# Four equal column strips in an elastic down-projection, and the expert attention's third and tail transposes moved ahead of V

## What is computed

```
m_small = sum(gumbel_weights[i] * _mlp_branch(ns2, w_fc1, b_fc1, w_fc2, b_fc2, C // ALPHA[i]) for i in range(3))
# _mlp_branch keeps the first C // ALPHA[i] = 192, 96, 64 channels at its input and at its output
h = jax.nn.gelu(xp * cmask @ w1 + b1, approximate=False)
return (h @ w2 + b2) * cmask
```

```
for e in range(wq.shape[0]):
    q = (x @ wq[e].T).reshape(b, s, nh, hd).transpose(0, 2, 1, 3)      # k, v alike
    scores = jnp.where(mask, jnp.einsum('bhqd,bhkd->bhqk', q, k) * scale, NEG)
    o = jnp.einsum('bhqk,bhkd->bhqd', jax.nn.softmax(scores, axis=-1), v)
    outs.append(o.transpose(0, 2, 1, 3).reshape(b, s, h) @ wo[e].T)
fused = jnp.concatenate(outs, axis=-1)
return jax.nn.silu(fused @ w_gate.T) * (fused @ w_up.T)
```

## Time and profile before

| | us |
|---|---|
| median of 3 runs | 1318.52 (1316.98 to 1318.92) |
| profiled execution | 1316.51 |
| its span (first to last instruction) | 1314.8 |
| mean granted TensorE clock | 0.922 of full |
| busy in the span: PE / PEld | 1190.5 (91%) / 939.6 (71%) |
| busy: ACT / DVE / POOL | 762.4 (58%) / 718.5 (55%) / 390.1 (30%) |

### The profile page before, as it was taken

One profiled execution on the slowest core, in us unless ns is written; L12 is line 12 of the kernel. 1 busy time (PEld: TensorE's weight loads), 2 busy tenths in 40 slices (PEclk: granted clock), 3 DMA queues, 4 the chain that ended last, 5 costly groups with the idle time before them and its releaser, 6 DMA issues. The chain is left out here.

```text
span 1314.8 us, 33568 instructions
## 1 busy us (share of the span) xinstructions
PE 1190.5 (91%) x13067; PEld 939.6 (71%) x13067; DVE 718.5 (55%) x2290; ACT 762.4 (58%) x3342; POOL 390.1 (30%) x529
## 2 busy tenths in 40 slices
PE   6789986999997699986899999999999999996898
PEld 5479954777774264324788898988889898883376
DVE  7345465666765113224667666666666666665200
ACT  1154534777773633313877777777777777873511
POOL 1100023433331433202443443444344344331000
PEclk8779976999997699966999999999999999996699
DMA  7000000000005300001000000000000000000000
GB/s 237 22 1 1 1 1 0 2 2 2 2 2 116 72 1 0 1 0 43 2 3 2 2 2 3 2 2 2 3 2 2 2 2 2 2 2 1 0 27 28
DMA packets 34732, 19.82 MB, mean 15 GB/s; under 512 B 24592, under 2 KB 32016, under 8 KB 34576
## 3 DMA queue, kind: packets, MB, share of 16 engines
q1 hardware_dynamic: 34432, 17.20, 4.9%
q10 hardware_dynamic: 144, 0.49, 0.1%
HBM read 15.12 MB, written 1.77 MB: 13 GB/s over the span
## 5 line engine op out<-in xcount | busy, mean ns | idle before, releaser
L1860 POOL TENSOR_TENSOR e_W<-e_W,e_RS 128x384 f32<-128x384 f32 x256 | 203.8, 827 | 348.7 <-DVE e_RS L1788 348.7
L1731 ACT ACTIVATE e_W<-banks,e_MX 128x128 f32<-128x128 f32 x768 | 268.9, 389 | 18.6 <-DVE e_MX L1776 18.5
L1731 ACT ACTIVATION_READ_ACCUMULATOR e_W<-banks,e_MX 128x1 f32 x768 | 175.9, 229 | 0.0
L1725 ACT COPY e_PT<-banks 128x512 f32<-128x512 f32 x128 | 69.0, 588 | 104.9 <-PE banks L1636 104.9
L1588 PE MATMUL banks<-XT,e_wqk 128*128 128x141 f32 x768 | 111.5, 296 | 11.8 <-DVE e_GU L1830 8.4
L1588 PEld LDWEIGHTS banks<-XT,e_wqk 128*128 128x128 f32 x768 | 97.8, 193 | 14.2 <-issue 11.6
L1636 PE MATMUL banks<-ident,e_W 128*128 128x128 f32 x768 | 105.5, 273 | 2.8 <-POOL e_W L1860 1.7
L1600 PE MATMUL banks<-e_wv,XT 128*128 128x192 f32 (+1 forms) x512 | 100.3, 339 | 0.1
L1636 PEld LDWEIGHTS banks<-ident,e_W 128*128 128x128 f32 x768 | 90.2, 141 | 6.3 <-POOL e_W L1860 2.0
L469 POOL TENSOR_TENSOR rstd<-veps,nhalf 128x6 f32<-128x6 f32 x15 | 20.6, 1372 | 242.6 <-DVE veps L435 242.6
L1117 POOL TENSOR_TENSOR f_W<-f_W,f_RS 128x423 f32<-128x423 f32 x64 | 56.3, 891 | 116.6 <-DVE f_RST L1101 108.7
(11 more groups left out here) (252 smaller groups left out, 2660.2 us busy)
## 6 DMA issues: line engine op xcount, KB each, us to landing
xp<-in_patches_dram SPq DMA_DIRECT2D x4, 768.0 KB, 8.6
H<-in_h_dram SPq DMA_DIRECT2D x1, 1728.0 KB, 10.8
out_dram<-H SPq DMA_DIRECT2D x6, 288.0 KB, 2.3
e_g<-in_e_gu_dram SPq DMA_DIRECT2D x1, 1536.0 KB, 8.1
e_o<-in_e_o_dram SPq DMA_DIRECT2D x4, 192.0 KB, 5.8
e_wqk<-in_e_qk_dram SPq DMA_DIRECT2D x8, 96.0 KB, 2.5
e_wqk<-in_e_qk_dram SPq DMA_DIRECT2D x24, 32.0 KB, 2.4
e_wv<-in_e_v_dram SPq DMA_DIRECT2D x4, 192.0 KB, 2.7
```

Of the source, the lines that this page charges most:

```text
L1725: nc.scalar.copy(PT[:, 4 * u:4 * u + 4, :], bank[4 + u][:, 0:4 * P]).then_inc(s_pa, 1)
L1731: ex = nc.scalar.activation(W[n % 2][:, t, :], bank[i][:, x * P:(x + 1) * P], ACT.Exp, bias=MX[:, t:t + 1], accum_out=SM[n % 2][:, t:t + 1])
L1860: nc.gpsimd.tensor_tensor(x, x, RS[n % 2][:, 3 * i:3 * i + 3].unsqueeze(2).broadcast_to([P, 3, P]), ALU.mult).then_inc(s_nm, 1)
```

## The change

Three edits. In `elastic_down` the 64-column matmul of variant 2 becomes two of 32 columns, in strips 0 and 1, with the same moving data; variants 1 and 0 stay in strips 2 and 3. In PE's list of the expert attention `project_v(n)` moves from behind `scores(n)` to behind `transpose_tail(n - 1)`. In DVE's list `evacuate_tail(n - 1)` moves up to behind `evacuate_weights(n - 1)`, and `evacuate_v(n)` moves down to behind the first reciprocals.

```diff
-                            for v, lo, n in ((2, 0, 64), (1, 64, 32), (0, 96, 32)):
-                                nc.tensor.matmul(t0[lo:lo + n, 0:GT_], m_w2[:, m, lo:lo + n], hid[g % 2][:, 3 * m + v, :],
+                            for v, lo in ((2, 0), (2, HP), (1, 2 * HP), (0, 3 * HP)):
+                                nc.tensor.matmul(t0[lo:lo + HP, 0:GT_], m_w2[:, m, lo:lo + HP], hid[g % 2][:, 3 * m + v, :],
                                                  start=(m == 0), stop=(m == HM - 1), tile_position=(0, lo),
                                                  skip_group_check=True)
...
                         if n < N:
                             scores(n)
-                            project_v(n)
                         if 1 <= n <= N:
                             pe.wait_ge(s_pa, 2 * n - 1)
                             pe.wait_ge(s_nm, 5 * n - 1)
...
                             transpose_tail(n - 1)
+                        if n < N:
+                            project_v(n)
                         if n >= 2:
                             out_project(n - 2)
...
                             maxima(n)
-                            evacuate_v(n)
                         if 1 <= n <= N:
                             evacuate_weights(n - 1)
+                            evacuate_tail(n - 1)
                         if n < N:
                             reciprocals(n, 0, 6, 2)
-                        if 1 <= n <= N:
-                            evacuate_tail(n - 1)
+                            evacuate_v(n)
```

## The result

The changed kernel takes 1284.18 us (median of 4 runs, 1278.96 to 1284.51) against 1318.35 us for the kernel before (4 runs, 1316.98 to 1318.92): a ratio of 0.9726, 95% interval 0.9702 to 0.9749, 2.7% faster. Forecast were 1289.6 us and a range of 1285 to 1298. The direction and both main mechanisms were right; the gain was larger, 34 us and not 29, and the time lies 0.8 us under the range. Of the 5.4 us, 3.5 are in the profiled spans (1314.8 to 1282.4, 32.4 less, where the sum had 28.9); the rest is that the sum put the median 2.0 us above the profiled execution (1.8 with the fourth run), where after the change it lay at it.

What follows compares the result with a forecast made beforehand. PE was taken to bound the elastic down-projections and expert attention. Savings of 14.2 + 3.0 + 11.7 = 28.9 us took the profiled 1316.51 to 1287.6; the median stands 2.0 higher, giving 1289.6 us, range 1285 to 1298.

Steps and rivals of the forecast that it cites:

- The strips: Elastic down-projections: four 32-column strips run together, a pair of blocks costs 2.21 us instead of 3.79, saving 14.2 us.
- The estimate from the Trainium skill's ratio for three strips: Elastic down: at 2.38 times instead of 3, a pass costs 0.42 us, saving 11 us; left out of the sum.
- The tail's wait: Expert attention: PE's wait at attend for DVE's tail-weights copy goes, 0.36 us in 31 short rounds, 11.2 us.
- V behind the transposes: Attention, PE: a transpose replaces V's matmul behind the tail scores, paying 56 ns extra against 104; 48 ns 63 times, 3.0 us.
- Rival A: Attention: DVE's V copy, blocked by POOL's multiplications, delays the q/k projection 2.5 us in 63 rounds; about 1445 us; 2%.
- Rival B: Elastic down: the fourth strip does not overlap the other three, 11.7 us more, 1301.3 us; 8%.
- Rival C: Attention: a new wait replaces the tail's at attend in short rounds, 11.2 us of gain missing, 1300.8 us; 12%.
- Rival D: Whole kernel: moments of PE clock change shift when a stage shortens, a few us either way, 1284 to 1295 us; 8%.
- The range: Whole kernel: 1285 (transposes pay nothing, kinder clock) to 1298 us (half of the new attend wait, or poorer strip overlap).

Runs made afterwards that it cites:

- a1_strips: The kernel before with the column-strip edit in elastic_down alone; 1301.71 us, ratio 0.9880 to the kernel before.
- c2_changed: The changed kernel measured again with nothing altered, beside the kernel before; 1284.54 us, ratio 0.9734 to the kernel before.
- b1_all32: The changed kernel with L1366's pair of 64-column matmuls also cut into four strips of 32; 1285.22 us, ratio 0.9748 to the kernel before.

## Why the prediction was right or wrong

- **The strips** (14.2 us): right, 14.1 in the changed kernel and in a1_strips. Four strips of 384 columns run together as `attend`'s did. (The last pass before L1366 costs 0.44 and not the 0.41 taken from a change the other way; hence 2.22.) The estimate from the Trainium skill's ratio for three strips (TensorE: Matmul & The Clock Gate, section "Measured speedup vs the span model") would have left 11; this trace does not agree, as a set of four strips costs 0.32 us, what one 64-column pass costs.
- **The tail's wait** (0.36 in 31 short rounds): right. `attend` follows after 0.21. It was close: DVE was 0.06 us ahead of PE and not 0.2, as the tail's copy took 0.31 us (0.27 before) and PE came 0.11 earlier than forecast.
- **V behind the transposes** (48 ns a round, 3.0 us): the step that failed. It said of V's own waits that they "get later to meet", taking them as met and pricing them at nothing; but V waited in every round for ACT's copy of k. That wait cost 0.06 of a later start and 0.06 in the first pass, its weights having been held back too: 0.115 a round, some 7 us over the stage, which went with the move. The 48 ns themselves came true, by luck. The forecast read V's 104 ns and the transposes' 56 ns as prices of the place behind the tail scores. But 58 of the 104 and all of the 56 are the price of a wait; they drop out of the difference, and what is left is V's price for the place, 0.047, while the transposes pay nothing there (109 ns a first pass, as any other). (In its new place V's first pass pays 0.02, the output projection 0.02 less than it did; these cancel, as forecast.)
- **A wait left out**: of PE's waits I weighed the tail's, k's, and V's, but not the second transposes' wait for DVE's copy of the attended output. With the short round 0.52 us shorter it became the last to arrive, and takes 0.09 us back there in every second round. Short rounds were forecast at 8.28 and are 8.16; long ones, which begin with that wait, 8.98 and 8.96: 0.16 - 0.09 = 0.07 is all they gained on 9.03. Per two rounds 0.59 us went where 0.46 was forecast, 4 us over the stage. In c2_changed's profile all of it shows, 18.6 us where 14.7 were forecast; in the first profile of the changed kernel the longer stay of the first two rounds at the lower clock level took 1.5 of them back.
- **Rival A** (V's copy late): out. The copy ends at 886.46 and the next q/k projection starts at 887.24. V's copies last 310 to 346 ns beside POOL's products (342 to 357 before). POOL's products take 822 to 832 ns, as before. So the lock that the Trainium skill describes (SBUF — State Buffer, section "SBUF: two separate sides") does not act on this copy from PSUM. **Rival B** is out by a1_strips. **Rival C** did come, at another place than named, and small. **Rival D** is seen as scatter of 1 or 2 us in single stretches, and once of 6 us ahead of the elastic stage (b1_all32).
- **The range**: its lower end took the transposes at "nothing" as the best case, a gain of 6.6 us at most from a price of 104 ns. With 0.16 us a round the same line reads 10.1 us, and the time 1282.5; with the 2.8 us of the wait left out it is 1285.3, 1.1 above the median measured.

## What to carry to other kernels

When a list of waits shows none, look at the starts: an instruction that starts 0.05 us behind the end of another engine's work, round after round, is waiting for it, even where pipelining hides the idle time. Moving independent work into that gap pays twice, for the gap and for the weight load that the wait held back. To price a wait and a place apart, look for a round, the first or the last, in which the one is there without the other. And after each gain compute the margin of every wait on the engine that sets the pace, not of those the change touches alone, for the next one may stand 0.1 us behind.

## What was not expected of the hardware

A matmul released by ACT's copy starts 0.052 to 0.054 us behind the copy's end, one released by DVE's copy of the attended output 0.055 to 0.058 us, and its first pass costs 0.056 us (transposes) or 0.058 us (V) more than one in the same place that had no wait. The list of waits shows nothing of it. Apart from that, V's first pass costs 0.209 us behind the tail scores, 0.183 behind the tail's transposes and 0.163 behind its own kind. And changing the column width costs PE about 0.1 us at the last pass (0.42 to 0.44 instead of 0.32) and 0.02 to 0.05 at the first: six sets of equal width took 1.93 to 1.96 us, where the same work with one change to 64 columns and back took 2.22.
